# One transpose of 16 columns instead of four of 4 for the score maxima of a group, and shift rows in 16 partitions

## The chip, the cores and the metric

The kernel runs on one core of a Trainium2 chip. The metric is the device time of one execution in microseconds (us); lower is better.

## The reference, cut to what matters

A transformer layer over 16 sequences of 512 tokens and 256 channels, 16 heads of 16 channels. Attention with a pre-norm comes first, then a mixture of experts, which the change doesn't touch.

```python
qkv = layernorm(x) @ W_attn + b_attn            # x: (16, 512, 256)
q, k = rope(q), rope(k)                         # q, k, v: (B, 16, 512, 16)
att = einsum('bhqd,bhkd->bhqk', q, k) / sqrt(hd)
att = where(causal, att, -inf)
att = softmax(att, axis=-1)
y = einsum('bhqk,bhkd->bhqd', att, v)
x = x + y @ W_proj + b_proj
x = x + moe(layernorm(x))                       # 8 experts, top 2, and a shared one
```

## The kernel before

Attention is a pipeline over batches (one sequence each, `b`), in each batch over four groups of four heads (`g`, NG = 4, GH = 4; G = 4b + g counts them, 64 in all), and in each group over five slots (`s`, UN = 5). A slot of TensorE holds the scores of one unit (two heads, or pieces of them, in the two banks of `pair_s`), the shifted scores of a unit of an earlier group, and pieces of the other work, which tables such as QK, QK_HIGH, PROJ and XN_T place at (group, slot). Each engine runs its own copy of this order; the engines meet at counting semaphores.

The softmax needs each row's maximum before the exponential. So scores are computed twice:

- `scores` (L1675, L1695): q.k with the causal mask into `pair_s`, released by DVE's last maxima.
- `row_max` on DVE (L1165 to L1171): maxima over keys into `mx`, 128 queries of a tile in the partitions, [NT, GH] in the free dimensions (NT = 4 tiles of 128 queries).
- `maxima` on TensorE (L1709), in slot 0 of the next group, behind that slot's shifted scores: four transposes turn `mx` into `ps_m[0:4, 0:512]`, a row for each head.
- `shift_rows` on ACT (L893), in slot 1, ahead of that slot's exponential: scales that and writes it as `m_row`, four partitions of 512 in f16.
- `load_shift` on SyncE (L477 waits, L480 issues), in slot 2: four DMAs, one a head, put each row into a partition (48 or 112) of `q_op`.
- `shifted` on TensorE (L1723), from slot 3 on: q.k again with the extra row, so that the maximum is subtracted in the product, into `pair_t`. ACT takes the exponential (L884) into `prob`, POOL zeroes what lies above the diagonal (L702), and `mix` (L1749) multiplies with the values.

Beside it in the same slots run the next batch's normalised input (transposes L1606), its q, k and v projections (L1615), whose q and k results ACT and DVE split in two f16 parts (`qkh` L861, `qkl` L1077) before SyncE stores them to DRAM (L458) and loads them again as `q_op` and `k_op` (L472, twelve DMAs for each half of a batch), and the last batch's output: its transposes L1765 and L1773, the projection L1784 into the same bank as the transposed maxima (it waits for `m_done`), the residual (L1194) and its stores (L511, L512).

SyncE's queue is in order: a shift row stands behind whatever stores and loads the tables put ahead of it, and behind their waits (L465 waits for a store to land).

Of the kernel before, what the change touches and what calls it, by code (L numbers as in the profile page):

```python
# [6 lines left out]
F32 = mybir.dt.float32  # L7
F32R = mybir.dt.float32r
F16 = mybir.dt.float16
BF16 = mybir.dt.bfloat16  # L10
I32 = mybir.dt.int32
ALU = mybir.AluOpType
ACT = mybir.ActivationFunctionType
AX_X = mybir.AxisListType.X
RMAX = bass.bass_isa.ReduceOp.max

P = 128
# [3 lines left out]
SHIFT_UNIT = 32768.0  # L21
# [18 lines left out]
def some(value):  # L40

    return not isinstance(value, int) or value > 0


def build(nc, x, w_attn, b_attn, w_proj, b_proj, ln_scale, ln_bias, gate_w, Wg, Wu, Wd, sWg, sWu, sWd, rope, out):
    NTOK, C = x.shape
    T = 512
    NB = NTOK // T
    NT = T // P
    H = 16  # L50
    HD = C // H
    GH = 4
# [34 lines left out]
    with ExitStack() as ctx:  # L87
        def sb(name, shape, dt):
            return ctx.enter_context(nc.sbuf_tensor(name, shape, dt))
# [3 lines left out]
        def sb_a(name, shape, dt):  # L93

            return ctx_a.enter_context(nc.sbuf_tensor(name, shape, dt))

        def sem(name):
            return ctx.enter_context(nc.semaphore(name))

        pair_s = ctx.enter_context(nc.psum_tensor("pair_s", [P, 2, 512], F32))  # L100
# [3 lines left out]
        ps_s, ps_t, ps_o, ps_q, ps_m, ps_y = bank[0:2], bank[2:4], bank[4], bank[5], bank[6], bank[7]  # L104
# [6 lines left out]
        ident = sb("ident", [P, P], F32)  # L111
# [46 lines left out]
        qkl = sb_a("qkl", [P, 4, T], F16)  # L158
        q_op = sb_a("q_op", [P, 2, H // 2, T], F16)
        k_op = sb_a("k_op", [P, 2, H // 2, T], F16)  # L160
        m_row = sb_a("m_row", [GH, 2, T], F16)
        v_op = sb_a("v_op", [P, 2, NT, H, 32], F32)
        mx = sb_a("mx", [P, 2, NT, GH], F32)
        prob = sb_a("prob", [P, 2, UN, 2, 512], F32)
        o_t = sb_a("o_t", [P, 2, NG, T], F32)
        rec = sb_a("rec", [P, 2, H], F32)
# [94 lines left out]
        S = {n: sem(n) for n in names}  # L261
# [184 lines left out]
        def _(sp):  # L446
# [27 lines left out]
            def load_shift(G, par, g):  # L474

                sp.wait_ge(S["m_done"], G + 1)
                sp.sem_inc(S["sp_passed"], 1)  # L477
                for h in range(GH):
                    row = 64 * (h % 2) + KR
                    sp.dma_start(q_op[row:row + 1, par, 2 * g + h // 2, :], m_row[h:h + 1, g % 2]  # L480
                                 ).then_inc(S["mrow_in"], 16)

            sp.dma_start(wa[:, 0:2, :], w_attn.rearrange("(k p) n -> p k n", p=P)).then_inc(S["w_in"], 16)
# [31 lines left out]
            def body(b, par, cur, prev, prev2, nxt, nxt2):  # L515
                if nxt2:
                    sp.wait_ge(S["xn_done"], b + 1)
                    sp.sem_inc(S["sp_passed"], 1)
                    load_x(b + 2, par)
                for g in range(NG):  # L520
                    G = 4 * b + g
                    has1 = (cur or g < 1) and (prev or g >= 1)
                    for s in range(UN):
                        if s == M_SP and has1:
                            load_shift(G - 1, par if g >= 1 else 1 - par, (g - 1) % 4)
                        for j in range(2):
                            late = QK_LOW[2 * j + 1] < QK[2 * j + 1]
                            n, there = (b, cur and prev) if late else (b + 1, nxt)
                            npar = par if late else 1 - par
                            if there and (g, s) == QK_STORE[j]:  # L530
                                store_qk(n, npar, j)
                            piece = UN * g + s - (UN * QK_LOAD[j][0] + QK_LOAD[j][1])
                            if there and 0 <= piece < 6:
                                load_qk(n, npar, j, piece // 2, piece % 2)
                        if prev and (g, s) == XRES:
                            if some(2 * (b - 1)):
                                sp.wait_ge(S["x1_done"], 2 * (b - 1))
                                sp.sem_inc(S["sp_passed"], 1)
                            sp.dma_start(xres[:], xv[b - 1]).then_inc(S["res_in"], 16)
                        for j, bp in halves_here((g, s), ROWS_OUT, b, prev, prev2):  # L540
                            store_half(bp, j)
# [296 lines left out]
        def _(act):  # L838
# [49 lines left out]
            def shift_rows(G, half):  # L888

                act.wait_ge(S["m_in"], G)  # L890
                if some(G - 2):
                    act.wait_ge(S["mrow_in"], MROWS * (G - 2))
                nc.scalar.activation(m_row[:, half], ps_m[0:GH, :], ACT.Copy, scale=1.0 / SHIFT_UNIT  # L893
                                     ).then_inc(S["m_done"], 1)

            def residual_high(bp, j):
# [7 lines left out]
            def body(b, par, cur, prev, prev2, nxt, nxt2):  # L904
                for g in range(NG):
# [3 lines left out]
                    for s in range(UN):  # L909
# [3 lines left out]
                        if s == M_ROWS and has1:  # L913
                            shift_rows(G, (g - 1) % 2)
# [122 lines left out]
            last = 2 * DBL + SINGLE - 1  # L1037
# [3 lines left out]
        def _(dve):  # L1041
# [115 lines left out]
            def row_max(G, g, u):  # L1157

                dve.wait_ge(S["s_in"], UN * G + u + 1)
                if u == 0:  # L1160
                    if some(G - 1):
                        dve.wait_ge(S["m_in"], G - 1)
                dst = mx[:, g % 2]
                if u < 2:
                    last = nc.vector.tensor_reduce(dst[:, 3, 2 * u:2 * u + 2], pair_s[:], AX_X, ALU.max)  # L1165
                elif u < 4:
                    c = 2 * (u - 2)
                    nc.vector.tensor_reduce(dst[:, 2, c:c + 2], pair_s[:, :, 0:384], AX_X, ALU.max)  # L1168
                    last = nc.vector.tensor_reduce(dst[:, 0, c:c + 2], pair_s[:, :, 384:512], AX_X, ALU.max)
                else:  # L1170
                    last = nc.vector.tensor_reduce(dst[:, 1].rearrange("p (c a) -> p a c", a=2),  # L1171
                                                   pair_s[:].rearrange("p a (c n) -> p a c n", c=2), AX_X, ALU.max)
                last.then_inc(S["max_done"], 1)

# [95 lines left out]
            def body(b, par, cur, prev, prev2, nxt, nxt2):  # L1270
                for g in range(NG):
                    G = 4 * b + g
                    for s in range(UN):
# [3 lines left out]
                        if cur:  # L1277
                            row_max(G, g, s)
# [316 lines left out]
        def _(pe):  # L1595
# [103 lines left out]
            def maxima(b, G, g):  # L1699

                pe.wait_ge(S["max_done"], UN * G)
                if some(G - 1):
                    pe.wait_ge(S["m_done"], G - 1)
                for j in range(2):
                    if g == (PROJ_B[j][0] + 1) % NG:
                        if some(2 * (b - 2) + j + 1):
                            pe.wait_ge(S["x1_done"], 2 * (b - 2) + j + 1)
                for q in range(NT):
                    last = nc.tensor.transpose(ps_m[0:GH, P * q:P * (q + 1)], mx[:, (g - 1) % 2, q, :], ident[:])  # L1709
                last.then_inc(S["m_in"], 1)  # L1710

            def shifted(G, par, gg, u):

# [75 lines left out]
            def body(b, par, cur, prev, prev2, nxt, nxt2):  # L1789
                for g in range(NG):  # L1790
# [3 lines left out]
                    for s in range(UN):  # L1794
# [6 lines left out]
                        if s == MAXIMA and has1:  # L1801
                            maxima(b, G, g)
# [256 lines left out]
```

## Time and profile before

| | us |
|---|---|
| median of 3 runs | 1797.29 |
| lowest, highest | 1796.71, 1798.85 |
| profiled execution | 1802.63 |
| its span, from first to last instruction | 1800.9 |
| TensorE busy | 1636.0 (91%) |
| DVE busy | 1169.6 (65%) |
| ACT busy | 874.3 (49%) |
| mean granted TensorE clock | 0.976 of full |

Busy times are sums over the whole span. Rows below are from the one profiled execution; a time at the start of a row counts from the start of its span. PE is TensorE's matmuls and PEld its weight loads, SP is SyncE, whose rows are issues of DMAs. What stands in brackets is how long the engine was idle before, and what ended that. In the chain of waits each piece was released by the piece before it.

### The profile page before, as it was taken

The page shows a single profiled execution, that of the slowest core. Times are in us where ns is not written, and L with a number is a line of the kernel's source. Part 1 is how long each engine was busy: PE and PEld are TensorE (multiplying, and loading weights), DVE is VectorE, ACT ScalarE, POOL GpSimd, SP SyncE. Part 2 cuts the span into 40 slices and gives each one's busy share as a digit, 9 for nine tenths or more (in the row PEclk, how much of TensorE's full clock was granted, in tenths as well). Part 3 has the DMA queues.
Part 4 walks back from the last instruction along what each step waited for, and adds up shares of the span by engine and source line. Part 5 has one row for each costly group of instructions (what it writes and reads, how often), then busy time and mean ns, then how long its engine had stood idle before and what let it go on. Part 6 is the DMA issues. An engine that isn't in the chain of part 4 may idle for free.

```text
span 1800.9 us, 45470 instructions
## 1 busy us (share of the span) xinstructions
PE 1636.0 (91%) x15505; PEld 1132.7 (63%) x15507; DVE 1169.6 (65%) x2062; ACT 874.3 (49%) x1273; POOL 780.0 (43%) x1005
## 2 busy tenths in 40 slices
PE   2689999999999999984798999989999999999996
PEld 2345555555555555432575566669999999999985
DVE  5568888888888888874358777874434444443442
ACT  1266666666666666552333222544444444444442
POOL 1023333333333333332200676725666666666652
PEclk9799999999999999987899999999999999999998
DMA  1322333333333333211536553223434333333432
GB/s 58 106 84 83 107 106 107 106 99 101 104 106 107 107 99 96 91 54 43 187 124 185 171 164 88 83 89 54 68 59 66 62 62 66 61 64 61 65 60 25
DMA packets 168709, 163.37 MB, mean 91 GB/s; under 512 B 29682, under 2 KB 159218, under 8 KB 168563
## 3 DMA queue, kind: packets, MB, share of 16 engines
q1 hardware_dynamic: 138354, 125.66, 22.8%
q0 software_dynamic: 30208, 35.81, 12.4%
q8 instruction: 86, 1.41, 0.3%
q14 instruction: 61, 0.49, 0.1%
HBM read 100.82 MB, written 60.30 MB: 89 GB/s over the span
## 4 chain that ended last, share of the span: by engine, by line
PE 68%; DVE 12%; issue 7%; DMA 5%; SPq 4%; ACT 3%; POOL 1%; DVEq 0%; POOLq 0%; ACTq 0%
PE bank L1615 21%; PE pair_s L1980 10%; PE pair_s L1615 7%; PE bank L1980 5%; PE pair_t L1980 5%; PE bank L1749 4%; PE pair_s L1675 3%; SPq L480 2%; PE pair_t L1723 2%; DVE mx L1165 2%; PE pair_t L1969 2%; ACT qkh L861 2%; SPq L472 1%; DMA q_op<-m_row 1%; PE bank L1765 1%
## 5 line engine op out<-in xcount | busy, mean ns | idle before, releaser
L884 ACT ACTIVATE prob<-pair_t 128x1024 f32<-128x1024 f32 x320 | 327.4, 1023 | 243.0 <-PE pair_t L1723 238.3
L702 POOL TENSOR_SCALAR_AFFINE_SELECT prob<-prob 128x256 f32<-128x256 f32 (+1 forms) x448 | 196.8, 453 | 478.0 <-ACT prob L884 466.4
L818 POOL DMA_INDIRECT out_x<-ysb,tok_rows x136 | 218.2, 1605 | 196.2 <-ACT ysb L1025 146.3
L1573 DVE SCALAR_TENSOR_TENSOR early<-pair_s,h_s,sg 128x512 f32<-128x512 f32 (+1 forms) x72 | 51.9, 721 | 249.0 <-PE pair_s L1980 249.0
L780 POOL DMA_INDIRECT tok_d<-tok_w,dest_i x128 | 126.6, 989 | 160.2 <-DVE dest_i L1424 121.5
L1980 PE MATMUL pair_s<-xt,wbuf 128*128 128x256 f16 (+1 forms) x1728 | 193.9, 267 | 1.9 <-DVE xt L1564 1.9
L1615 PE MATMUL bank<-wbuf,early 128*128 x1632 | 190.2, 273 | 0.9 <-ACT ysb L1025 0.8
L1749 PE MATMUL bank<-prob,v_op 128*32 128x512 f32 (+3 forms) x2048 | 181.5, 450 | 2.0 <-POOL prob L702 1.7
L1016 ACT CAST early<-early 128x512 f16<-128x512 f32 (+1 forms) x144 | 85.6, 594 | 196.6 <-DVE early L1573 196.6
L1615 PE MATMUL pair_s<-wsh,xt 128*128 128x512 f16 x768 | 179.2, 382 | 0.0
L1980 PEld LDWEIGHTS pair_s<-xt,wbuf 128*128 x1728 | 163.0, 98 | 22.3 <-issue 2.3
L1165 DVE TENSOR_REDUCE mx<-pair_s 128x2 f32<-128x1024 f32 x128 | 155.9, 1218 | 25.8 <-PE pair_s L1695 25.1
L799 POOL DMA_INDIRECT xrow<-xhl_d,tok_rows x136 | 136.5, 1003 | 74.3 <-issue 37.8
L1615 PEld LDWEIGHTS bank<-wbuf,early 128*128 128x128 f16 x1632 | 155.8, 98 | 19.6 <-issue 1.5
L1675 PE MATMUL pair_s<-k_op,q_op 48*128 48x512 f16 (+3 forms) x1024 | 127.6, 307 | 35.6 <-DVE mx L1165 13.9
L1675 PEld LDWEIGHTS pair_s<-k_op,q_op 48*128 48x128 f16 x1024 | 34.8, 94 | 155.4 <-DVE mx L1165 79.0
L1168 DVE TENSOR_REDUCE mx<-pair_s 128x2 f32<-128x768 f32 x128 | 121.8, 952 | 16.4 <-PE pair_s L1695 15.2
L1579 DVE TENSOR_TENSOR early<-early 128x512 f16<-128x512 f32 (+1 forms) x144 | 95.3, 662 | 55.1 <-ACT early L1016 49.6
L1723 PE MATMUL pair_t<-q_op,k_op 49*128 49x512 f16 (+3 forms) x1024 | 123.9, 299 | 6.6 <-DMA q_op<-m_row 4.1
L1615 PEld LDWEIGHTS pair_s<-wsh,xt 128*128 128x128 f16 x768 | 74.5, 98 | 75.3 <-issue 1.7
L1025 ACT ACTIVATE ysb<-bank,row_w 128x256 f32<-128x256 f32 x136 | 64.4, 473 | 87.9 <-PE bank L1615 87.8
L1980 PE MATMUL bank<-xt,wbuf 128*128 128x256 f16 (+1 forms) x864 | 103.2, 267 | 0.0
(259 smaller groups left out, 3090.8 us busy)
## 6 DMA issues: line engine op xcount, KB each, us to landing
q_op<-qk_d SPq DMA_DIRECT2D x192, 64.0 KB, 2.4
k_op<-qk_d SPq DMA_DIRECT2D x192, 64.0 KB, 2.4
x_in<-in_L_attn_x SPq DMA_DIRECT2D x16, 512.0 KB, 4.2
qk_d<-qkh SPq DMA_DIRECT2D x32, 256.0 KB, 2.5
qk_d<-qkl SPq DMA_DIRECT2D x32, 256.0 KB, 2.7
xres<-in_L_attn_x SPq DMA_DIRECT2D x16, 512.0 KB, 4.7
x_d<-x SPq DMA_DIRECT2D x32, 256.0 KB, 2.2
xhl_d<-xhl SPq DMA_DIRECT2D x32, 256.0 KB, 2.5
```

The lines of the kernel that those rows point to most:

```text
L702: last = nc.gpsimd.affine_select(out=v, in_=v, compare_op=ALU.is_ge, fill=0.0, base=0, pattern=[[0, v.shape[1]], [1, P]], channel_multipli ...
L780: pool.indirect_dma_start(out=tok_d, out_offset=bass.IndirectOffsetOnAxis(ap=dest_i[:, t, k:k + 1], axis=0), in_=tok_w[:, t, k, :], in_off ...
L799: pool.indirect_dma_start(out=xrow[:, k % GATHERED], out_offset=None, in_=xhl_d, in_offset=bass.IndirectOffsetOnAxis(ap=tok_rows[:, k, 0:1 ...
L818: pool.indirect_dma_start(out=out, out_offset=bass.IndirectOffsetOnAxis(ap=tok_rows[:, k, 0:1], axis=0), in_=ysb[:, k % ROWS_AHEAD], in_of ...
L884: nc.scalar.activation(prob[:, half, u].rearrange("p a n -> p (a n)"), pair_t[:].rearrange("p a n -> p (a n)"), ACT.Exp, scale=exp_by).the ...
L1165: last = nc.vector.tensor_reduce(dst[:, 3, 2 * u:2 * u + 2], pair_s[:], AX_X, ALU.max)
L1168: nc.vector.tensor_reduce(dst[:, 2, c:c + 2], pair_s[:, :, 0:384], AX_X, ALU.max)
L1615: last = nc.tensor.matmul(out, a, m, start=(i == 0), stop=(i == n - 1))
L1675: nc.tensor.matmul(ps_s[a][:, lo:lo + P * (q + 1)], q_op[64 * a:64 * a + KR, par, pair, P * q:P * (q + 1)], k_op[64 * a:64 * a + KR, par, ...
L1723: last = nc.tensor.matmul(ps_t[a][:, lo:lo + n], k_op[rows, par, pair, P * k:P * (k + 1)], q_op[rows, par, pair, P * k:], start=start, sto ...
L1749: last = nc.tensor.matmul(ps_o[32 * h:32 * h + 32, P * k:], v_op[:, vpar, k, GH * gg + h, :], pr[:, unit, h % 2, lo:lo + n], start=(piece ...
L1980: last = nc.tensor.matmul(out[:, w * k:w * k + w], wbuf[:, a], xt2[:, par, x, 0:w], start=(i == 0), stop=(i == 3 * CC - 1))
```

## The change

The maxima are laid out head first ([GH, NT] instead of [NT, GH]), so that one transpose of 16 columns turns all four tiles of a group. The result has 16 partitions (4 x head + tile) of 128 instead of four of 512. The copy on ACT takes and writes that shape, and each of the four DMAs reads four partitions of 256 bytes and writes the same row of `q_op` as before. No step changes its place in any engine's order, and no wait is added or removed.

```diff
--- before.py
+++ after.py
@@ -158,9 +158,9 @@
         qkl = sb_a("qkl", [P, 4, T], F16)
         q_op = sb_a("q_op", [P, 2, H // 2, T], F16)
         k_op = sb_a("k_op", [P, 2, H // 2, T], F16)
-        m_row = sb_a("m_row", [GH, 2, T], F16)
+        m_row = sb_a("m_row", [NT * GH, 2, P], F16)
         v_op = sb_a("v_op", [P, 2, NT, H, 32], F32)
-        mx = sb_a("mx", [P, 2, NT, GH], F32)
+        mx = sb_a("mx", [P, 2, GH, NT], F32)
         prob = sb_a("prob", [P, 2, UN, 2, 512], F32)
         o_t = sb_a("o_t", [P, 2, NG, T], F32)
         rec = sb_a("rec", [P, 2, H], F32)
@@ -477,7 +477,7 @@
                 sp.sem_inc(S["sp_passed"], 1)
                 for h in range(GH):
                     row = 64 * (h % 2) + KR
-                    sp.dma_start(q_op[row:row + 1, par, 2 * g + h // 2, :], m_row[h:h + 1, g % 2]
+                    sp.dma_start(q_op[row:row + 1, par, 2 * g + h // 2, :], m_row[NT * h:NT * h + NT, g % 2, :]
                                  ).then_inc(S["mrow_in"], 16)
 
             sp.dma_start(wa[:, 0:2, :], w_attn.rearrange("(k p) n -> p k n", p=P)).then_inc(S["w_in"], 16)
@@ -890,7 +890,7 @@
                 act.wait_ge(S["m_in"], G)
                 if some(G - 2):
                     act.wait_ge(S["mrow_in"], MROWS * (G - 2))
-                nc.scalar.activation(m_row[:, half], ps_m[0:GH, :], ACT.Copy, scale=1.0 / SHIFT_UNIT
+                nc.scalar.activation(m_row[:, half], ps_m[0:NT * GH, 0:P], ACT.Copy, scale=1.0 / SHIFT_UNIT
                                      ).then_inc(S["m_done"], 1)
 
             def residual_high(bp, j):
@@ -1162,13 +1162,13 @@
                         dve.wait_ge(S["m_in"], G - 1)
                 dst = mx[:, g % 2]
                 if u < 2:
-                    last = nc.vector.tensor_reduce(dst[:, 3, 2 * u:2 * u + 2], pair_s[:], AX_X, ALU.max)
+                    last = nc.vector.tensor_reduce(dst[:, 2 * u:2 * u + 2, 3], pair_s[:], AX_X, ALU.max)
                 elif u < 4:
                     c = 2 * (u - 2)
-                    nc.vector.tensor_reduce(dst[:, 2, c:c + 2], pair_s[:, :, 0:384], AX_X, ALU.max)
-                    last = nc.vector.tensor_reduce(dst[:, 0, c:c + 2], pair_s[:, :, 384:512], AX_X, ALU.max)
+                    nc.vector.tensor_reduce(dst[:, c:c + 2, 2], pair_s[:, :, 0:384], AX_X, ALU.max)
+                    last = nc.vector.tensor_reduce(dst[:, c:c + 2, 0], pair_s[:, :, 384:512], AX_X, ALU.max)
                 else:
-                    last = nc.vector.tensor_reduce(dst[:, 1].rearrange("p (c a) -> p a c", a=2),
+                    last = nc.vector.tensor_reduce(dst[:, :, 1].rearrange("p (c a) -> p a c", a=2),
                                                    pair_s[:].rearrange("p a (c n) -> p a c n", c=2), AX_X, ALU.max)
                 last.then_inc(S["max_done"], 1)
 
@@ -1705,9 +1705,8 @@
                     if g == (PROJ_B[j][0] + 1) % NG:
                         if some(2 * (b - 2) + j + 1):
                             pe.wait_ge(S["x1_done"], 2 * (b - 2) + j + 1)
-                for q in range(NT):
-                    last = nc.tensor.transpose(ps_m[0:GH, P * q:P * (q + 1)], mx[:, (g - 1) % 2, q, :], ident[:])
-                last.then_inc(S["m_in"], 1)
+                nc.tensor.transpose(ps_m[0:NT * GH, 0:P], mx[:, (g - 1) % 2].rearrange("p h t -> p (h t)"), ident[:]
+                                    ).then_inc(S["m_in"], 1)
 
             def shifted(G, par, gg, u):
```

## Rows read from the trace of the kernel before

**Rows 1.** The page: its first line, and part 4, the chain by engine and line.
```profile
span 1800.9 us, 45470 instructions
...
PE 68%; DVE 12%; issue 7%; DMA 5%; SPq 4%; ACT 3%; POOL 1%; DVEq 0%; POOLq 0%; ACTq 0%
PE bank L1615 21%; PE pair_s L1980 10%; PE pair_s L1615 7%; PE bank L1980 5%; PE pair_t L1980 5%; PE bank L1749 4%; PE pair_s L1675 3%; SPq L480 2%; PE pair_t L1723 2%; DVE mx L1165 2%; PE pair_t L1969 2%; ACT qkh L861 2%; SPq L472 1%; DMA 
```

**Rows 2.** Windows: engines' busy time (instructions), granted clock, DMA share, GB/s.
```profile
389.00:436.00 47.00, 45.14 (x462) 24.63 (x461) 41.27 (x78) 32.19 (x44) 17.88 (x37) 1.00 0.34 103
718.00:765.00 47.00, 43.25 (x441) 23.19 (x440) 38.48 (x65) 28.54 (x37) 16.12 (x34) 1.00 0.30 91
765.00:812.00 47.00, 37.00 (x369) 16.19 (x370) 33.97 (x62) 27.93 (x35) 17.00 (x35) 0.89 0.17 52
```

**Rows 3.** Timeline, group 2: start, us, engine, line, [idle before <- releaser].
```profile
408.82 0.38 PE L1723 MATMUL pair_t<-q_op,k_op 49*128 49x384 f16 x4
409.14 0.60 PE L1709 MATMUL bank<-ident,mx 128*4 128x128 f32 x4
409.25 1.02 ACT L884 ACTIVATE prob<-pair_t 128x1024 f32<-128x1024 f32 x1 [1.34 <-PE pair_t L1723]
410.17 0.68 ACT L861 ACTIVATE qkh<-bank,bcol 128x512 f16<-128x512 f32 x1
410.88 0.75 DVE L1077 SCALAR_TENSOR_TENSOR qkl<-bank,bcol,qkh 128x512 f16<-128x512 f32 x1 [0.63 <-ACT qkh L861]
411.69 0.39 PE L1615 MATMUL bank<-wah,xh 128*128 128x256 f32 x1 [0.35 <-DVE qkl L1077]
```

**Rows 4.** Timeline, TensorE: where it waits in groups 0, 1 and 3.
```profile
388.50 0.63 PE L1606 MATMUL bank<-ident,xn 128*128 128x128 f32 x4 [0.31 <-DVE qkl L1077]
...
400.91 0.12 PEld L1675 LDWEIGHTS pair_s<-k_op,q_op 48*128 48x128 f16 x4 [0.46 <-DVE mx L1165]
...
423.15 0.51 PE L1615 MATMUL bank<-xh,wah 128*128 128x512 f32 x1 [0.35 <-DVE qkl L1077]
```

**Rows 5.** Tile mx: the transposes; duration ns min/median/max.
```profile
L1709 PE MATMUL bank<-ident,mx x256: 269/272/418, 73.8 to 804.2; 128*4 128x128 f32 x128
```

**Rows 6.** Tile m_row: copy, issues, who waited for it (us, times), landing.
```profile
L480 SPq DMA_DIRECT2D q_op<-m_row x256: 497/589/1628, 75.5 to 807.0; - x128
L893 ACT ACTIVATE m_row<-bank x64: 569/569/587, 74.8 to 804.6; 4x512 f16<-4x512 f32 x64
...
  PEld pair_t L1723: 6.8, 13
...
DMA to landing us min/median/max: 1.6/1.7/3.8
```

**Rows 7.** Lines from 60 to 807 us: xcount | busy us, mean ns | idle before.
```profile
L884 ACT ACTIVATE prob<-pair_t 128x1024 f32<-128x1024 f32 x314 | 321.2, 1023 | 229.6 <-PE pair_t L1723 224.9
L925 ACT COPY o_t<-bank 128x512 f32<-128x512 f32 x62 | 36.0, 581 | 0.0
```

**Rows 8.** Other issues on SyncE: line L472, and a piece of the timeline.
```profile
L472 SPq DMA_DIRECT2D q_op<-qk_d x192: 303/426/1772, 47.9 to 773.5; - x192
...
1.56 0.32 SPq L485 DMA_DIRECT2D early<-in_L_attn_b_attn  x1
```

**Rows 9.** The chain (start, us, what), then timeline rows around group 0's start.
```profile
410.85 0.46 ACT m_row L893
...
427.58 0.10 PEld L1723 LDWEIGHTS pair_t<-q_op,k_op 49*128 49x128 f16 x2 [0.25 <-DMA q_op<-m_row]
...
430.09 1.23 DVE L1171 TENSOR_REDUCE mx<-pair_s 128x4 f32<-128x1024 f32 x1
...
431.43 0.12 PEld L1675 LDWEIGHTS pair_s<-k_op,q_op 48*128 48x128 f16 x2 [0.51 <-DMA k_op<-qk_d]
```

**Rows 10.** Timeline, weight loads: waits on the way into the drain.
```profile
753.13 0.10 PEld L1723 LDWEIGHTS pair_t<-q_op,k_op 49*128 49x128 f16 x2 [1.29 <-DMA q_op<-m_row]
...
778.35 0.10 PEld L1675 LDWEIGHTS pair_s<-k_op,q_op 48*128 48x128 f16 x2 [1.82 <-DMA k_op<-qk_d]
```

## The prediction, made before the changed kernel was run

> **What bounds the kernel now.** I read the page first. Its chain of waits gives 68% of the span to TensorE and 12% to VectorE, and its list by line shows no piece of L1709, the line of the transposes that the change thins out; it does show the shift row's issue L480, and ACT's L861 and DVE's L1165, at about 2% each [rows 1]. The change touches attention alone, whose last maxima are transposed at about 804 us; behind it nothing changes.
>
> The windows come next. In a steady stretch of 47 us TensorE is busy 45.14 us, DVE 41.27, ACT 32.19, at a clock of 1.00 [rows 2]. That looks like a TensorE bound, under which every matmul removed would be time won. A busy share alone doesn't decide it, so I looked at where TensorE stands still behind the transposes, in each of the four groups of one batch.
>
> Group 2 of the batch, first [rows 3]. TensorE issues the shifted scores of slot 0 at 408.82, then the four transposes at 409.14, then the value products, then slot 1. But at 411.69 it starts the next q/k projection only when DVE's qkl L1077 has emptied the bank, and stands idle 0.35 us for it. That qkl ran from 410.88 to 411.63; it followed ACT's qkh at 410.17, which followed the exponential of 409.25, which followed the shifted scores of 408.82. Everything on that chain starts from work that is issued ahead of the transposes. Whatever they free, TensorE then waits longer at 411.69.
>
> The other three groups show the same [rows 4]. In group 3 TensorE waits 0.35 us for qkl at 423.15. In group 1 it waits 0.46 us for DVE's maxima at 400.91, and by the program those stand in DVE's queue behind the qkl of slot 0. In group 0 it waits 0.31 us for qkl at 388.50. So in a steady batch no group passes the shortened time on.
>
> **The change, part by part.** *The transposes.* Four of 128x4 become one of 128x16. One takes 272 ns [rows 5] and the four together 0.60 us [rows 3], so each of the three removed is worth (0.60 - 0.27) / 3 = 0.11 us of TensorE, 0.33 us a group, 21 us over the 64 groups. The moving operand is the same identity of 128 columns, so I price the remaining one at 0.27. Of these 21 us I put steady groups (about 60) at nothing, because of the waits above: the cover is the ACT and DVE chain, and if it were gone the 21 us would show. At the two ends of attention, where TensorE doesn't stay full (765 to 812 us: 37.00 of 47 us, clock 0.89 [rows 2]), the transposes can be on the chain; with some four groups and 0.33 to 0.6 us each (the slower clock makes them dearer), I take 1.5 us. Bounds: 0 and 21.
>
> *The copy on ACT* (L893) takes 569 ns for 4x512 [rows 6]. Its cost goes by columns: 128x512 takes 581 and 128x1024 takes 1023 [rows 7], so 442 ns for 512 columns, and 128 columns would take 581 - 384 x 0.863 = 250 ns. It saves 0.32 us at each group. The other side: nothing, if a fixed part dominates. I take 0.3. ACT itself has room [rows 2]; what the copy also sets is when SyncE may issue the shift rows.
>
> *The shift rows' DMAs* (L480). Still four a group, each 1 KB into one row of q_op; now the source is 4 partitions of 256 bytes, before it was one of 1 KB. They are the dearest of SyncE's regular issues: 589 ns median, where q_op and k_op loads take 426 [rows 6, 8], so 2.4 us a group. Nothing in the trace has the new form. The nearest rows are itself (589), the loads from many rows (426), and L485, a single row of 3 KB, 0.32 us as the first of its burst, where L472's shortest is 0.303 and L480's is 0.497. From below: 0.16 us less for each. From above: 0.16 us more, an estimate that mirrors the distance between the two kinds, for a source and destination of unlike shape. I take 589 unchanged, since both sides stay in SBUF and the bytes are the same. Landing (1.6 to 3.8 us, median 1.7 [rows 6]) I leave too.
>
> The Trainium skill bears on this: DMA: Bandwidth & Descriptors, section "Why a DMA increments its semaphore by 16 and not by 1", says that such a copy is spread over the largest number of engines, up to 16, that divides both outer sizes, and that the issuing sequencer itself writes the increments of the unused ones. By that rule the new copy goes over 4 engines with 12 increments written by SyncE, which speaks for a dearer issue; the page gives no price on this chip, and no run here shows the split yet. At the upper bound above the sum would come to rival 2's instead.
>
> *Where this path is late.* SyncE's queue runs from the copy at 410.85 over four issues, two stores of results, the q/k stores, eight loads and four more shift-row issues, to the shifted scores at 427.58, which waited 0.25 us [rows 9]. The k_op loads behind it make TensorE wait till 431.43, but there DVE's maxima (430.09 + 1.23) end at 431.32, so only 0.1 us of that can be won. In all TensorE waits for shift rows 6.8 us, 13 times [rows 6]; the mean is 0.52. The shorter copy takes at most 0.3 off each, 3.9 us. Some waits are shorter than that, and behind 427.58 DVE's own queue is nearly as late, so I take 2.5. Into the drain the waits are larger, 1.29 at 753.13 and 1.82 at 778.35 [rows 10], with several copies in series on the way: another 1 us.
>
> **Sum**, against the profiled execution of 1802.6 us (span 1800.9 and 1.7 around it), 5.3 above the median of 1797.3: -1.5 (transposes at the ends) - 2.5 (shift rows in steady batches) - 1 (drain) = -5. So 1792.3 for the median, 0.28% faster.
>
> **Rivals.**
> 1. *TensorE is the bound after all* and the transposes count in full: 64 x 0.33 = 21 us, and the 5 us less its first term: 1773. For it: 45.14 of 47 us busy. Against it: the four waits of rows 3 and 4.
> 2. *The issue gets dearer*, which decides for slower. With 0.16 us more an issue, eight issues stand ahead of 427.58, +1.3 us less 0.3 of the copy, so about 1 us a batch where the path is already even with TensorE. 16 batches less some slack: 12 us slower, 1809. It turns at 0.3 / 8 = 0.04 us an issue. For it: the source is four rows and the destination one. Against: single-row L485 was cheap [rows 8]. The skill's rule named above speaks for it too.
> 3. *The issue gets cheaper*, down to 426: the waits for shift rows and a part of those of the drain go, another 4 us: 1788.
> 4. *Nothing to see*: the copy keeps its fixed cost, or DVE's queue takes back what the shift rows win. 1796, within 0.2%.
> 5. *The clock falls* since TensorE idles 1.3 us more a batch. At 43.25 of 47 busy it still had 1.00 [rows 2], and I expect about 43.8; so it would be at most some 0.4 us a batch, 1803.
>
> **How the numbers follow.** A measurement of this kernel can tell about 0.2% from no change, 3.6 us. Chances: my forecast 0.37, cheaper issue 0.15, full transposes 0.06, nothing 0.26, dearer issue 0.11, clock 0.05. The forecast's own spread (1789 to 1796) puts part of it, some 0.07, within 0.2%, and part of the dearer issues would be small. So faster 0.51, same 0.35, slower 0.14. Range: from 1786, which takes in the cheaper issue, to 1801, which takes in nothing and a slightly dearer issue; the far tails, some 0.17, are left out.
>
> **What the profile would show.** Right: L1709 at 64 instructions, the copy near 250 ns, and TensorE's waits for qkl L1077 longer by 0.3 us in three groups of each batch, so that busy time falls by some 17 us and the span by 5. The waits for q_op<-m_row fall from 6.8 us towards 3. Wrong: the waits for qkl don't grow and the period of a batch falls by 1.3 us (rival 1); or L480's median moves off 589 ns and the waits for m_row and k_op with it (rivals 2 and 3). The weakest step is the price of the new issue, which I have from no row, and the next is how much slack SyncE's path has in the batches that show no wait.

## The result and the profile after

The changed kernel took 1792.58 us (median of 16 runs, 1789.54 to 1821.11), the kernel before 1799.61 in 16 runs beside it (1796.71 to 1803.78). The ratio is 0.9961, 95% interval 0.9951 to 0.9971: 0.39% faster, or 7.0 us between the medians, where 0.28% and 5 us were forecast; the interval of the measurement reaches from 0.29 to 0.49%. The 1821.11 is a single run at a lower granted clock (0.926, the others 0.972 to 0.977) and is left out of the ratio.

The page of the changed kernel, its first line and the chain of waits, answers to [rows 1]. SyncE's issues held 4% of the chain and DMA 5%; now 1% and 2%:

```profile
span 1793.9 us, 45086 instructions
...
PE 71%; DVE 15%; issue 7%; ACT 3%; DMA 2%; SPq 1%; POOL 1%; DVEq 0%; POOLq 0%; ACTq 0%
```

The tiles `mx` and `m_row` of the changed kernel, against [rows 5] and [rows 6] (durations are ns, min/median/max; then the first and the last start in us):

```profile
L1708 PEld LDWEIGHTS bank<-ident,mx x64: 87/88/89, 73.0 to 795.0; 128*16 128x16 f32 x64
L1708 PE MATMUL bank<-ident,mx x64: 269/277/382, 73.1 to 795.0; 128*16 128x128 f32 x64
```

```profile
L480 SPq DMA_DIRECT2D q_op<-m_row x256: 572/573/712, 73.8 to 797.7; - x128
L893 ACT ACTIVATE m_row<-bank x64: 248/250/266, 73.4 to 795.5; 16x128 f16<-16x128 f32 x64
...
who waited for it (us, times):
```

The transpose of 16 columns costs what one of four did, 277 against 272 ns. ACT's copy takes 250 ns where I had worked out 250. The issue's median went from 589 to 573, but the shortest, which was the first of a burst, from 497 to 572, so that the usual burst of four is as long as before (2.40 us then, 2.43 now). The longest issue went from 1628 to 712 ns. And nobody waits for a shift row any more: the list of who waited is empty, where it had 13 weight loads and 6.8 us.

The same place in group 2 as in [rows 3], from the timeline of the changed kernel:

```profile
408.61 0.38 PE L1722 MATMUL pair_t<-q_op,k_op 49*128 49x384 f16 x4
408.93 0.28 PE L1708 MATMUL bank<-ident,mx 128*16 128x128 f32 x1
```

```profile
409.04 1.02 ACT L884 ACTIVATE prob<-pair_t 128x1024 f32<-128x1024 f32 x1 [1.34 <-PE pair_t L1722]
409.96 0.68 ACT L861 ACTIVATE qkh<-bank,bcol 128x512 f16<-128x512 f32 x1
```

```profile
410.67 0.75 DVE L1077 SCALAR_TENSOR_TENSOR qkl<-bank,bcol,qkh 128x512 f16<-128x512 f32 x1 [0.63 <-ACT qkh L861]
```

```profile
411.48 0.39 PE L1615 MATMUL bank<-wah,xh 128*128 128x256 f32 x1 [0.68 <-DVE qkl L1077]
...
422.95 0.50 PE L1615 MATMUL bank<-xh,wah 128*128 128x512 f32 x1 [0.68 <-DVE qkl L1077]
```

And in group 1, where TensorE waits for maxima instead (0.46 us at 400.91 in [rows 4]):

```profile
400.69 0.12 PEld L1675 LDWEIGHTS pair_s<-k_op,q_op 48*128 48x128 f16 x4 [0.78 <-DVE mx L1165]
```

From the shifted scores to the q/k projection it took 2.87 us before (408.82 to 411.69) and takes 2.87 now (408.61 to 411.48). The transposes between them are 0.33 us shorter, and TensorE's wait is 0.33 us longer: 0.68 where 0.35 stood, here and in group 3. In group 1 it is 0.32 us longer, and in group 0 the 13 waits of the transposes L1606 for qkl went from 3.5 to 7.8 us in all, 0.33 us each. The windows say it as a sum, against the first of [rows 2]: TensorE's busy time in the same 47 us fell by 1.26 us, and the clock stayed.

```profile
389.00:436.00 47.00, 43.88 (x456) 23.88 (x458) 41.49 (x78) 30.86 (x43) 18.21 (x37) 1.00 0.33 102
765.00:812.00 47.00, 34.61 (x338) 15.11 (x336) 31.19 (x59) 25.29 (x32) 17.75 (x37) 0.91 0.16 48
```

Where then do the 7 us of span come from? The first and the last start of the turned maxima bound the attention stage: 73.8 to 804.2 before [rows 5], 730.4 us; 73.1 to 795.0 now, 721.9 us. Attention won 8.5 us, and 1.5 of these were lost again outside that stretch, where nothing was changed: 0.7 us were won ahead of it and 2.2 lost behind it.

### The profile page after: what moved, and what is told of

Same layout as the page of the kernel before. It is cut to its first block, busy times and chain, and to the rows that moved or that the text cites. A ratio compares the mean times of both kernels' runs of the same rounds, so it can differ in the third digit from the quotient of the medians.

```text
span 1793.9 us, 45086 instructions
## 1 busy us (share of the span) xinstructions
PE 1617.9 (90%) x15313; PEld 1123.6 (63%) x15315; DVE 1168.4 (65%) x2062; ACT 855.3 (48%) x1273; POOL 780.0 (43%) x1005
## 4 chain that ended last, share of the span: by engine, by line
PE 71%; DVE 15%; issue 7%; ACT 3%; DMA 2%; SPq 1%; POOL 1%; DVEq 0%; POOLq 0%; ACTq 0%
PE bank L1615 23%; PE pair_s L1979 10%; PE pair_s L1615 7%; PE bank L1979 5%; PE pair_t L1979 5%; PE bank L1748 5%; PE pair_s L1675 4%; DVE mx L1165 3%; PE pair_t L1722 2%; PE bank L1764 2%; PE pair_t L1968 2%; ACT qkh L861 2%; DVE mx L1168 2%; DVE qkl L1077 1%; DVE xhl L1227 1%
```

## The experiments

They ran on three other chips: t_again, copy_long, form_only and copy_short on one, the qkh_first and max_first kernels on the second, form_16, stats_later and the repeats on the third. The medians of the kernel before were 1965.8, 1964.3 and 1962.6 us there. Its repeat has 1962.8 us of span, because the expert part, behind attention, takes some 160 us longer than on the first chip; attention took the same time, as the repeats of the two kernels show. Each ratio is against runs of the kernel before on the same chip. Beside it I read the stretch from the first to the last start of the turned maxima; that is one profile of each kernel, and the profile of the kernel before that it is held against is the repeat's, from the third chip.

**Repeats of both kernels** (before_again and after_again).

> The kernel before, unchanged, on the chip of the experiments, for its trace: waits for shift rows 5 to 8 us as on the first chip, batches of 46.1 us.

> The changed kernel, unchanged, on the chip of the experiments, for its trace: no waits for shift rows, batches of 46.1 us, attention 3 to 9 us shorter than before_again.

The tile `mx` of the kernel before, and then of the changed one, on this chip:

```profile
L1709 PE MATMUL bank<-ident,mx x256: 269/272/417, 73.5 to 804.1; 128*4 128x128 f32 x128
```

```profile
L1708 PE MATMUL bank<-ident,mx x64: 269/277/381, 72.2 to 793.0; 128*16 128x128 f32 x64
```

That is 730.6 and 720.8 us (spans 1962.8 and 1955.5): 9.8 us won in attention, where the first pair of profiles had 8.5. The two profiles of one kernel differ by 0.2 us before and 1.1 us after; with two of each, the true scatter can be larger (the five runs of qkh_first_b below lie 9.3 us apart). The waits for shift rows were 8.8 us in 15 weight loads, a little over the 5 to 8 expected, and none in the changed kernel, as expected. That attention is 9.8 us shorter is just past the 3 to 9 that I had written. The batches were expected at 46.1 us. The twelve from the third on took 46.4 us on average before and 45.9 in the changed kernel; but before they range from 46.0 to 47.0 us, and in the changed kernel all lie within 0.06 us of 45.9. So a batch that nothing disturbed was as long before as now, to 0.1 us: the gain lies in the batches that had come late.

**Do the transposes count?** The changed kernel, with its one transpose issued four times:

```diff
-                nc.tensor.transpose(ps_m[0:NT * GH, 0:P], mx[:, (g - 1) % 2].rearrange("p h t -> p (h t)"), ident[:]
-                                    ).then_inc(S["m_in"], 1)
+                for q in range(NT):
+                    last = nc.tensor.transpose(ps_m[0:NT * GH, 0:P],
+                                               mx[:, (g - 1) % 2].rearrange("p h t -> p (h t)"), ident[:])
+                last.then_inc(S["m_in"], 1)
```

> The changed kernel, with its one transpose of 16 columns issued four times into the same place, so that TensorE does as much as before (4 x 0.11 us a group) while the shift rows go the new way. Theory 1 (TensorE's time here is covered by the ACT and DVE chain in steady batches, and counts only at the ends): 0.9965 of before, within 2 us of the changed kernel, and TensorE's waits for qkl shrink back. Theory 2 (the transposes bring the gain): the gain is gone, 0.999 to 1.001.

Measured 0.9967, interval 0.9956 to 0.9978. Tile `mx`, and from the list of waits TensorE's for qkl, first of this kernel, then of the changed one, then of the kernel before:

```profile
L1709 PE MATMUL bank<-ident,mx x256: 269/273/420, 72.4 to 794.8; 128*16 128x128 f32 x128
```

```profile
PEld bank L1615 <- DVE qkl L1077: 18.9, 30, 0.6
```

```profile
PEld bank L1615 <- DVE qkl L1077: 28.6, 30, 1.0
```

```profile
PEld bank L1615 <- DVE qkl L1077: 19.1, 30, 0.6
```

All the matmuls are back and the gain is still there: attention takes 722.4 us against the changed kernel's 720.8 and 721.9. The wait for qkl stood at 19.1 us for 30 waits, went to 28.6, and with the matmuls back is 18.9 again: 0.32 us at each wait, what the three transposes are worth. Theory 2 is out; the transposes' own part is between 0.5 and 1.6 us, near the scatter of two profiles. The period of a batch says the same: 45.96 us with four matmuls, 45.90 with one, 1 us over the whole of attention.

**The copy or the DMA's form?** Three kernels. `copy_long` is the changed kernel with a copy as long as before:

```diff
-        m_row = sb_a("m_row", [NT * GH, 2, P], F16)
+        m_row = sb_a("m_row", [NT * GH, 2, 4, P], F16)
...
-                nc.scalar.activation(m_row[:, half], ps_m[0:NT * GH, 0:P], ACT.Copy, scale=1.0 / SHIFT_UNIT
+                nc.scalar.activation(m_row[:, half], ps_m[0:NT * GH, 0:P].unsqueeze(1).broadcast_to([NT * GH, 4, P]),
+                                     ACT.Copy, scale=1.0 / SHIFT_UNIT
...
```

> The changed kernel, with ACT's copy reading the 128 columns four times and writing 512, so that it takes about 0.57 us again; one transpose and the new DMA form stay. If the shorter copy carries the gain of steady batches and the drain (my sum: 0.3 us on each late shift row): 0.998. If the new form of the DMA carries it: 0.9965 to 0.997, and TensorE still hardly waits for shift rows.

`form_only` is the kernel before, with each shift row kept as four pieces of 256 bytes:

```diff
-        m_row = sb_a("m_row", [GH, 2, T], F16)
+        m_row = sb_a("m_row", [GH, 2, NT, P + 8], F16)
...
-                    sp.dma_start(q_op[row:row + 1, par, 2 * g + h // 2, :], m_row[h:h + 1, g % 2]
+                    sp.dma_start(q_op[row:row + 1, par, 2 * g + h // 2, :].rearrange("p (a n) -> p a n", a=NT),
+                                 m_row[h:h + 1, g % 2, :, 0:P]
...
```

(ACT's copy writes its 4x512 into these pieces.)

> The kernel before with the DMA form alone changed: four transposes, a copy of 4x512 on ACT into rows with a gap behind each 128, and each DMA reads 4 pieces of 256 bytes. If the form (issue and landing) carries the gain: 0.997, and the waits for shift rows fall from 6.8 us to under 2. If the copy carries it: 0.999 to 1.0, waits about 6 us.

`copy_short` is the kernel before with a short copy:

```diff
+            nc.gpsimd.memset(m_row[:], 0.0)
...
-                nc.scalar.activation(m_row[:, half], ps_m[0:GH, :], ACT.Copy, scale=1.0 / SHIFT_UNIT
+                nc.scalar.activation(m_row[:, half, 0:P], ps_m[0:GH, 0:P], ACT.Copy, scale=1.0 / SHIFT_UNIT
```

> The kernel before with a copy of 4x128 on ACT instead of 4x512 (about 0.25 us), all else as before. It leaves out three quarters of the shift rows, which stay zero; the softmax then runs on unshifted scores there. If the shorter copy carries the gain: 0.998, waits for shift rows 3 us of 6.8. If the form does: 0.999 to 1.0.

| kernel | transposes | copy, ns | pieces of a shift row | ratio (95%) | first to last turned maxima, us | waits for shift rows, us (times) |
|---|---|---|---|---|---|---|
| before, repeated | 4 | 570 | one, 1 KB | 1 | 730.6 | 8.8 (15) |
| copy_short | 4 | 250 | one, 1 KB | 0.9978 (0.9966 to 0.9989) | 724.1 | 2.1 (4) |
| form_only | 4 | 569 | 4 of 256 B | 0.9976 (0.9963 to 0.9988) | 725.6 | 0.4 (2) |
| copy_long | 1 | 570 | 4 of 256 B | 0.9964 (0.9952 to 0.9977) | 725.0 | 0.8 (3) |
| t_again | 4 | 250 | 4 of 256 B | 0.9967 (0.9956 to 0.9978) | 722.4 | none |
| changed, repeated | 1 | 249 | 4 of 256 B | see above | 720.8 | none |

Their rows, one fence each, in the order `copy_short`, `form_only`, `copy_long`, with who waited for the row's landing; for `copy_long` they are from its list of waits:

```profile
L480 SPq DMA_DIRECT2D q_op<-m_row x256: 497/589/1357, 74.7 to 800.1; - x128
...
  PEld pair_t L1724: 2.1, 4
```

```profile
L480 SPq DMA_DIRECT2D q_op<-m_row x256: 567/573/722, 72.7 to 799.8; - x128
L894 ACT ACTIVATE m_row<-bank x64: 569/569/587, 72.1 to 797.3; 4x512 f16<-4x512 f32 x64
...
  PEld pair_t L1725: 0.4, 2
```

```profile
PEld pair_t L1723 <- DMA q_op<-m_row: 0.8, 3, 0.3
PE bank L1784 <- ACT m_row L893: 5.7, 13, 0.4
```

Either part alone gives a good half of it. By the ratios the copy wins 4.3 us (2.2 to 6.7) and the form 4.7 (2.4 to 7.3), both together 6.5 (4.3 to 8.6, t_again). By the stretches, one profile each, it is 6.5, 5.0 and 8.2. They work on the same waits: of 8.8 us the copy took away 6.7 and the form 8.4. The expectations named the copy or the form, and both held. The last fence shows what the long copy costs beyond SyncE: with the transpose shorter, the output projection (L1784), which writes the same bank, waits for the copy 13 times, 0.4 us each.

By the ratios alone, copy_long (0.9964) can't be told from t_again or form_only, and copy_short not from form_only. Any order among them rests on one profile of each.

**Is it the number of packets, or only the broken-up source?** As form_only, but in 16 pieces of 64 bytes:

```diff
-        m_row = sb_a("m_row", [GH, 2, T], F16)
+        m_row = sb_a("m_row", [GH, 2, 16, 48], F16)
...
-                    sp.dma_start(q_op[row:row + 1, par, 2 * g + h // 2, :], m_row[h:h + 1, g % 2]
+                    sp.dma_start(q_op[row:row + 1, par, 2 * g + h // 2, :].rearrange("p (a n) -> p a n", a=16),
+                                 m_row[h:h + 1, g % 2, :, 0:32]
...
```

> The kernel before, with each shift row kept in 16 pieces of 64 bytes with gaps, so that the DMA has a broken-up source as form_only had, but the packets stay 16 of 64 bytes as before. If the four larger packets are what took the waits for shift rows from 6.8 us to 0.4 in form_only: 0.999 to 1.0 here, waits 5 to 7 us, landing median 1.7 us. If the broken-up source alone did it: 0.998, waits under 2 us.

Measured 1.0002 (0.9991 to 1.0014). Its issues, its landing and its waits are again those of the kernel before ([rows 6], and 8.8 us in the repeat):

```profile
L480 SPq DMA_DIRECT2D q_op<-m_row x256: 497/589/1908, 73.5 to 805.1; - x128
...
  PEld pair_t L1725: 8.8, 16
...
DMA to landing us min/median/max: 1.6/1.8/3.6
```

The count of packets of form_16, which is also that of the repeat of the kernel before, and then of form_only, from the view of the DMA queues:

```profile
DMA packets 168708, 163.37 MB, mean 83 GB/s; under 512 B 29681, under 2 KB 159217, under 8 KB 168562
```

```profile
DMA packets 162564, 163.36 MB, mean 83 GB/s; under 512 B 23537, under 2 KB 153073, under 8 KB 162418
```

So the contiguous row had always gone as 16 small packets. In four pieces it needs 6144 fewer in all, 24 for each of 256 DMAs. The Trainium skill's rule (DMA: Bandwidth & Descriptors, "Why a DMA increments its semaphore by 16 and not by 1") gives just this: 4 engines in place of 16 are 12 packets of data and 12 increments fewer. The trace agrees with the count, and the sizes in its packet records say which: form_only has 4096 packets of 64 bytes fewer and 1024 of 256 bytes more, and 3072 of 4 bytes fewer. The dearer issue, for which I had let the rule speak, didn't come.

The packet records also show when the data of each row arrived, which the view of the tile leaves out for the new form. From the end of the issue to the end of the last data packet, the median is 0.80 us with 16 packets (repeat of the kernel before) and 0.72 us with four (form_only). The difference lies in the slow ones. In 29 of the 256 rows of the kernel before the last packet came over 1 us after the issue, up to 1.98 us, and in 26 of these 29 it was just one or two of the 16 packets that were so late. form_16 has 28 such rows, form_only one, the changed kernel one and, in its repeat, five. Ten of the 15 waits for shift rows, 7.3 of their 8.8 us, stand behind a burst of four with such a row. So form_16 rules out the broken-up source as the cause. It doesn't tell whether it is the fewer data packets or the fewer increments, that is the fewer engines, for both changed together.

**Is the chain over ACT and DVE the cover?** On ACT, qkh now goes ahead of the same slot's exponential, in the kernel before (qkh_first_b) and in the changed one (qkh_first_a):

```diff
+                        if nxt:
+                            for i in range(4):
+                                if (g, s) == QK_HIGH[i] and QK_HIGH[i] >= QK[i]:
+                                    qk_high(b + 1, i)
                         if s >= LAG - UN and has1:
                             exponentials(G - 1, s + UN - LAG, (g - 1) % 2)
...
-                            for i in range(4):
-                                if (g, s) == QK_HIGH[i] and QK_HIGH[i] >= QK[i]:
-                                    qk_high(b + 1, i)
```

> The kernel before, with ACT's qkh (L861) ahead of the same slot's exponential instead of behind it. Theory 1 says that the chain shifted scores, exponential, qkh, qkl sets the end of slots 0 and 1 in three groups of four. Taken off it, each of these groups can win up to the 0.35 us that TensorE waited: about 10 to 15 us in all, 0.992 to 0.995. If TensorE is the bound anyway, 1.0.

> The changed kernel with the same move of qkh. With the cover gone, the 0.33 us of the transposes come through in three groups of a batch, 45 in all, 15 us; on top of the changed kernel's 0.996 and what the move itself brings: 0.980 to 0.985, against the move alone at least 0.6% faster. If the transposes' time is covered by something else too, it stays within 0.4% of the move alone.

Measured 0.9900 (0.9882 to 0.9918) and 0.9825 (0.9809 to 0.9841). The quotient of the two is 0.9924, 15 us (some 10 to 20, an estimate from the two intervals): what the whole change brings once the cover is gone, about twice the 7 to 8 us that it brings with it. The move alone won 20 us (16 to 23; 1.0% of 1964), more than the 10 to 15 expected.

These 15 us are not the transposes alone, for qkh_first_b still waited 9.3 us for shift rows and qkh_first_a never. What the transposes bring is read from batches that nothing disturbed, from one start of the turned maxima to the same one a batch later, first in qkh_first_b, then in qkh_first_a (the three groups between are left out):

```profile
526.52 0.60 PE L1710 MATMUL bank<-ident,mx 128*4 128x128 f32 x4
571.22 0.60 PE L1710 MATMUL bank<-ident,mx 128*4 128x128 f32 x4
```

```profile
513.36 0.28 PE L1709 MATMUL bank<-ident,mx 128*16 128x128 f32 x1
557.45 0.28 PE L1709 MATMUL bank<-ident,mx 128*16 128x128 f32 x1
```

That is 44.70 and 44.09 us: 0.61 us a batch, 9 to 10 us over attention, where the kernels with the cover differ by 0.06. I had expected three groups of 0.33 us, 1.0 us a batch and 15 in all, on top of what the shift rows bring; it is as much as two groups. qkh_first_a is faster than both kernels: 1929.34 us median where the kernel before had 1964.25.

Two timelines of qkh_first_a, ACT and DVE: qkh fits into what was ACT's idle time ahead of the exponential, and qkl follows the maxima without a gap. In the chain of waits, below, the transpose stands as a link of its own, in this batch once more at 425.25, so in two of its four groups. In the chains of the kernel before and of the changed one it stands in no group of the steady batches from 200 to 700 us:

```profile
403.55 0.69 ACT L861 ACTIVATE qkh<-bank,bcol 128x512 f16<-128x512 f32 x1 [0.22 <-PE bank L1616]
404.16 1.02 ACT L884 ACTIVATE prob<-pair_t 128x1024 f32<-128x1024 f32 x1
```

```profile
403.94 1.23 DVE L1166 TENSOR_REDUCE mx<-pair_s 128x2 f32<-128x1024 f32 x1 [0.42 <-PE pair_s L1696]
405.08 0.74 DVE L1078 SCALAR_TENSOR_TENSOR qkl<-bank,bcol,qkh 128x512 f16<-128x512 f32 x1
```

```profile
403.90 0.22 PE pair_t L1723 x4
404.12 0.21 PE bank L1709
404.32 0.99 PE bank L1749 x8
```

**The transposes put on the chain.** The call of `maxima` moved ahead of slot 0's `shifted`, in the kernel before (max_first_b) and in the changed one (max_first_a):

```diff
+                        if s == MAXIMA and has1:
+                            maxima(b, G, g)
                         if s >= LAG - UN and has1:
                             shifted(G - 1, par if g >= 1 else 1 - par, (g - 1) % 4, s + UN - LAG)
...
-                        if s == MAXIMA and has1:
-                            maxima(b, G, g)
```

> The kernel before, with the transposes of the maxima ahead of slot 0's shifted scores instead of behind them. Theory 1: they are then on the chain to the exponential, four for 0.43 us in three groups a batch (45 to 48 groups) and in part in the fourth: 1.008 to 1.014. If the chain isn't what bounds: 1.0.

> The changed kernel with the one transpose ahead of slot 0's shifted scores. Theory 1: 0.11 us on the chain, about 5 us: 0.997 to 1.0, at least 0.8% below the same move in the kernel before. If the chain isn't what bounds, 0.996 as without the move.

Measured 1.0175 (1.0156 to 1.0194) and 1.0034 (1.0023 to 1.0045). The direction is that of theory 1, both sizes are above it. The first is 34 us over the kernel before, 0.54 us for each of 64 groups; I had expected 0.43 and in fewer groups. Its chain of waits has the transposes in 63 of the 64 groups, and 0.54 us is nearly the whole time of the four (0.60), where I had taken four times the 0.11 us at which they follow each other. The quotient is 0.9861, 27 us. An undisturbed batch of max_first_b and one of max_first_a, again from a start to the same one a batch later:

```profile
460.70 0.60 PE L1709 MATMUL bank<-ident,mx 128*4 128x128 f32 x4
508.87 0.60 PE L1709 MATMUL bank<-ident,mx 128*4 128x128 f32 x4
```

```profile
638.20 0.28 PE L1708 MATMUL bank<-ident,mx 128*16 128x128 f32 x1
685.10 0.28 PE L1708 MATMUL bank<-ident,mx 128*16 128x128 f32 x1
```

The period is 48.17 us with four transposes and 46.90 with one: 1.3 us, four groups of 0.33, 21 us over the kernel. The other 6 us are about what the shift rows bring in the kernels without the move, and here too their waits went, from 8.9 to 0.4 us.

**More of the same?** On top of qkh_first_a (stats_later), residual statistics of half 0 later:

```diff
-        X1, X1_STATS, X1_VARIANCE = ((3, 4), (1, 1)), ((0, 0), (1, 2)), ((0, 4), (2, 4))
-        RSTD_B, ROWS = ((0, 4), (3, 0)), ((1, 3), (3, 1))
+        X1, X1_STATS, X1_VARIANCE = ((3, 4), (1, 1)), ((1, 0), (1, 2)), ((1, 1), (2, 4))
+        RSTD_B, ROWS = ((1, 1), (3, 0)), ((1, 3), (3, 1))
```

> The changed kernel with qkh ahead of the exponential, and with the residual's statistics, variance and rstd of half 0 moved from group 0 to group 1 (slots 0, 1, 1). In group 0 TensorE waited 0.62 us for qkl behind these statistics (0.74 us on DVE). If DVE's order is what bounds group 0: 0.5 us a batch, 8 us, 0.978; if DVE then holds group 1 up by as much: 0.9825 as without.

Measured 0.9854 (0.9837 to 0.9871): no gain on 0.9825, rather a loss. TensorE's wait for qkl in group 0 (0.62 us in qkh_first_a) no longer stands in the timeline, but in group 1 it now waits 0.47 us for maxima, where it went through before, and in group 2 it waits 0.28 us as it did. DVE's work was moved, and its lateness with it; why this costs more than it gave is open:

```profile
388.83 0.39 PE L1676 MATMUL pair_s<-k_op,q_op 48*128 48x384 f16 x4 [0.47 <-DVE mx L1166]
400.88 0.39 PE L1676 MATMUL pair_s<-k_op,q_op 48*128 48x384 f16 x4 [0.28 <-DVE mx L1166]
```

## Why the prediction was right

**The steady batches give nothing for the transposes.** Right, to 0.06 us a batch, and shown from three sides: the wait for qkl took up 0.32 us at each of 30 places; putting the matmuls back cost at most 1.6 us of the 21 that they are worth; and with qkh moved, the undisturbed batch became 0.6 us shorter by the change. That the whole change brought 15 us there, the figure that I had worked out as 45 groups of 0.33 us for the transposes alone, is a coincidence: they gave 9 to 10 of them, and the shift rows' path the rest. Put on the chain (max_first) they came through in full, 1.3 us a batch. A busy share of 96% on TensorE, the base of rival 1, was no bound.

**The transposes at the two ends, 1.5 us.** Not refuted, and not shown: t_again is 0.5 to 1.6 us behind the two profiles of the changed kernel, about their scatter of 1.1, and 0.06 us a batch would already make 1 us of it.

**The copy, 0.3 us at each group.** Right: 569 to 250 ns. The slope by columns from [rows 7] held down to 128 columns.

**The shift rows' path, 2.5 + 1 us.** The path was the right one, the term too small: without the transposes' part it won 6.5 us by the ratio (4.3 to 8.6) and 8.2 by the stretch (730.6 to 722.4), where the sum had 3.5. The step that was wrong is the landing, which I had left as it was: the form alone took the waits from 8.8 to 0.4 us and won 4.7 us (2.4 to 7.3), by rows that no longer land late, while the usual burst of issues stayed as long as before. The median, which I went by, moved by less than 0.1 us; it was the slow rows that went, and how often a row came near the maximum of 3.8 us I hadn't asked. For the copy 3.5 us lie within what copy_short measured (2.2 to 6.7); only its single profile says 6.5. TensorE's waits for k_op, which stand behind the shift rows in SyncE's queue, fell as well, from 13.0 to 10.9 us and in the repeats from 12.0 to 10.2. How the gain divides between steady batches and the drain (the 1 us) isn't shown: the last three groups became 4.1 us shorter in the first pair of profiles and 0.8 in the second.

**The number.** The 5 us forecast and the 7 us measured are sums in which the part for the transposes wasn't confirmed and the part for the shift rows was about half of what it should be. That 1792.3 and 1792.58 agree so well is luck: the median of the kernel before was 1797.29 in the three runs known then and 1799.61 in 16.

**The rivals.** The dearer issue (0.11): no; the usual burst stays the same. The cheaper issue (0.15): no, but the same waits did vanish, by another way; it had priced them at 4 us more, and attention did come out 8.5 to 9.8 us shorter. The clock: 1.00 at 43.88 us busy, and 0.91 at the end of attention where it had been 0.89. "Nothing to see" is outside the interval.

**What stays open.** Why one or two of 16 packets come late, and whether it is fewer packets or fewer engines that spares the row such stragglers. And behind attention 2.2 us of what it wins are lost in the first pair of profiles and 3.8 in the second, in a part of the program that wasn't changed. The granted clock may be a part of it: from 1100 to 1300 us it was 1.00 before and 0.98 in the changed kernel, with nearly the same work (192.4 and 192.7 us busy), and over the whole span 0.976 and 0.972. No run tests that.

## What to carry to other kernels

Before an engine's instructions are priced as time, find its next wait behind them and ask where the chain that ends this wait began: if that is ahead of the instructions, they are free, and removing them only lengthens the wait. Then it pays to change what ends the wait; here one call moved on ACT won more than the change, and made the change worth about twice as much. Where a small transfer is waited for now and then, look at its slowest landings and not at the median: here the median moved by under 0.1 us and the waits nearly vanished. And when two experiments on the same kernel are divided by each other, the quotient holds all that differs between them; the period of an undisturbed batch says what one part of it is worth.

## What the runs showed of the hardware

A contiguous shift row of 1 KB from one partition to another went as 16 packets of 64 bytes; the same row in four pieces of 256 bytes went with 24 packets fewer (data and increments), and waits for it fell from 8.8 to 0.4 us. With 16 packets 29 of 256 rows had their last data over 1 us after the end of the issue, mostly for one or two packets; with four packets one row had (medians 0.80 and 0.72 us). The issue on SyncE took about 500 ns for the first and 589 for the next in a burst with 16 packets, and some 590 for the first and 573 for the later ones with four (form_only); a burst of four is 2.40 and 2.44 us.

A transpose of 128x16 f32 took 277 ns, one of 128x4 272, and those of 128x128 (L1765) 283 on average, all against the same identity of 128 columns: the number of columns that are turned hardly mattered.
